# The adapter's large weight in 16 half-megabyte loads paced by the LSTM's steps, and its bias loaded after the first step

## What is computed

```python
xz = einsum('ntd,dk->ntk', x, Wx) + b
def step((h, c), xz_t):
    ai, af, ao, ag = split(xz_t + h @ Wh, 4)
    c = sigmoid(af) * c + sigmoid(ai) * tanh(ag)
    h = sigmoid(ao) * tanh(c)
x = x + all h                                   # (16, 256, 256)

n = layernorm(cond) * gamma + beta
hid = gelu(n @ W1 + bias1)                      # (16, 256)
w = hid @ W2 + bias2                            # W2 is 256 x 8192: the large adapter weight
a1, b1, a2, b2 = [t.reshape(16, 256, 8) for t in split(w, 4)]
mid = gelu(x @ base_down + (x @ a2) @ b2.T)     # the rank-8 factors differ for each sequence
out = x + mid @ base_up.T + (mid @ b1) @ a1.T
```

## Time and profile before

| | |
|---|---|
| median of 3 runs (lowest to highest) | 608.72 us (607.85 to 609.86) |
| the profiled execution: its own time, its span | 610.4 us, 608.4 us |
| PE: matmuls busy, share, records | 589.4 us, 97%, 14092 |
| DVE, ACT, POOL busy | 476.1, 375.6, 49.6 us |
| mean granted TensorE clock | 0.992 of full |
| DMA: moved, mean rate | 39.73 MB, 65 GB/s |

### The profile page before, as it was taken

One profiled execution on the slowest core, in us unless ns is written; L12 is line 12 of the kernel. 1 busy time (PEld: TensorE's weight loads), 2 busy tenths in 40 slices (PEclk: granted clock), 3 DMA queues, 4 the chain that ended last, 5 costly groups with the idle time before them and its releaser, 6 DMA issues.

```text
span 608.4 us, 33942 instructions
## 1 busy us (share of the span) xinstructions
PE 589.4 (97%) x14092; PEld 437.7 (72%) x14092; DVE 476.1 (78%) x2549; ACT 375.6 (62%) x2154; POOL 49.6 (8%) x96
## 2 busy tenths in 40 slices
PE   8697999999999999999999999999999999999997
PEld 5564667777777777777777777777777777777886
DVE  2576787888888888888888888888888888888773
ACT  1364566666666666666666666666666666666663
POOL 5001320000000000000000000000000000000000
PEclk9799899999999999999999999999999999999999
DMA  7889340232322123333212233321223333123301
GB/s 193 218 222 307 62 59 13 38 56 56 56 56 39 39 37 56 55 56 56 42 38 34 56 56 55 55 48 34 34 54 56 56 55 53 32 31 46 56 20 29
DMA packets 32139, 39.73 MB, mean 65 GB/s; under 512 B 3905, under 2 KB 29809, under 8 KB 30962
## 3 DMA queue, kind: packets, MB, share of 16 engines
q1 hardware_dynamic: 31282, 36.51, 30.7%
q0 software_dynamic: 704, 1.05, 1.1%
HBM read 16.05 MB, written 4.19 MB: 33 GB/s over the span
## 4 chain that ended last, share of the span: by engine, by line
PE 95%; issue 1%; DMA 1%; POOL 1%; DVE 1%; SPq 0%; ACT 0%; POOLq 0%; ACTq 0%
PE z L676 36%; PE x_bank L480 19%; PE z_o L676 9%; PE aux L506 8%; PE out_bank L530 7%; PE aux L491 3%; PE aux L458 3%; PE out_bank L562 2%; PE aux L513 2%; PE out_bank L605 2%; DMA seed<-proj 1%; PE out_bank L551 1%; PE x_bank L551 1%; PE x_bank L506 0%; DMA x_nat<-in_x 0%
## 5 line engine op out<-in xcount | busy, mean ns | idle before, releaser
L676 PE MATMUL z<-wh,h_t 128*16 128x96 f32 x8160 | 237.2, 249 | 3.7 <-issue 3.3
L676 PEld LDWEIGHTS z<-wh,h_t 128*16 128x16 f32 x8160 | 152.8, 96 | 112.4 <-DVE h_t L849 80.4
L829 DVE STREAM_TRANSPOSE z<-z 128x96 f32<-128x96 f32 x512 | 152.6, 298 | 73.9 <-PE z L676 50.0
L401 ACT ACTIVATE gates<-z 128x48 f32<-128x48 f32 x512 | 107.6, 210 | 123.2 <-DVE z L829 123.0
L480 PE MATMUL x_bank<-wx,x_t 128*128 128x256 f32 x512 | 156.6, 394 | 0.5 <-ACT x_t L333 0.5
L339 ACT ACTIVATE z<-seed 128x96 f32<-128x96 f32 x512 | 127.5, 249 | 5.8 <-DMA seed<-proj 5.8
L676 PE MATMUL z_o<-wh,h_t 128*16 128x64 f32 x4080 | 104.9, 219 | 0.3 <-issue 0.3
L839 DVE SCALAR_TENSOR_TENSOR prod<-gates 128x32 f32<-128x32 f32 x512 | 98.1, 192 | 0.0
L343 ACT ACTIVATE z_o<-seed 128x64 f32<-128x64 f32 x256 | 58.3, 228 | 60.3 <-DVE h_t L849 60.3
L844 DVE SCALAR_TENSOR_TENSOR gates<-prod 128x16 f32<-128x16 f32 x512 | 84.6, 165 | 8.7
L480 PEld LDWEIGHTS x_bank<-wx,x_t 128*128 128x128 f32 x512 | 81.3, 197 | 6.0 <-issue 1.7
(11 more groups left out here) (123 smaller groups left out, 441.7 us busy)
## 6 DMA issues: line engine op xcount, KB each, us to landing
seed<-proj SPq DMA_DIRECT2D x128, 128.0 KB, 4.3
w<-in_L_cond_W SPq DMA_DIRECT2D x4, 2048.0 KB, 10.7
x_nat<-in_x SPq DMA_DIRECT2D x32, 128.0 KB, 4.3
out<-y_nat SPq DMA_DIRECT2D x32, 128.0 KB, 4.3
wx<-in_L_cond_Wx SPq DMA_DIRECT2D x2, 512.0 KB, 5.5
wh<-in_L_cond_Wh SPq DMA_DIRECT2D x2, 256.0 KB, 6.9
wh<-in_L_cond_Wh SPq DMA_DIRECT2D x1, 512.0 KB, 5.9
w_bias<-in_L_cond_bias POOLq DMA_DIRECT2D x4, 128.0 KB, 6.0
```

The source lines that it names most:

```text
L401: act.activation(gates[s % 2][m][:, 0:3 * B].rearrange("p (g b) -> p g b", b=B), zt[m].rearrange("p (g c) -> p g c", c=C)[:, :, 0:B], ACT. ...
L676: ins = pe.matmul(dst, h_prev[:, kc, :], rhs, start=False, stop=(kc == 1), skip_group_check=True)
L829: dve.transpose(zt[m], z_bank[m][:, 0:GC]).then_inc(turned[m], 1)
```

## The change

W2 is loaded in 16 pieces of 512 KB, one for each piece of work on PE, so that each piece has its own semaphore and PE waits for each. The first two (`W_AHEAD`) go out where the first quarter did. Of the others, piece p is issued once step p - 2 has its h. A piece is a half of the columns and a half of the contraction of a quarter; each of the 128 partitions gets four runs of 1 KB. The bias transfers of POOL now wait until step 0 has its h; they stand behind the `pow` of the layer norm (L959). The cut diff:

```diff
+W_AHEAD = 2
...
-        w2_loaded = [sem(f"w2_loaded{q}") for q in range(4)]
+        w2_loaded = [[sem(f"w2_loaded{q}_{i}") for i in range(NQ)] for q in range(4)]
...
-            w2_q = W2.rearrange("(k p) (q n) -> q p k n", p=P, q=4)
-            def load_w2(q):
-                sp.dma_start(w2[q][:, :, :], w2_q[q]).then_inc(w2_loaded[q], 16)
+            w2_parts = W2.rearrange("(k p) (q j h n) -> q h k p j n", p=P, q=4, j=NQ, n=W_HALF)
+            def load_w2(piece):
+                n, i = divmod(piece, NQ)
+                q, (h, kc) = QUARTERS[n], divmod(i, 2)
+                if piece == 3 * NQ:
+                    sp.wait_ge(w_psum, 2)
+                sp.dma_start(w2[q][:, kc, :].rearrange("p (j h n) -> p h j n", j=NQ, n=W_HALF)[:, h], w2_parts[q, h, kc])\
+                  .then_inc(w2_loaded[q][i], 16)
...
-            load_w2(QUARTERS[0])
+            for piece in range(W_AHEAD):
+                load_w2(piece)
             load_seed(Blk(0, 1))
...
-                if not k.at_least(1):
-                    load_w2(QUARTERS[1])
-                if k.k == 1:
-                    sp.wait_ge(w_psum, 2)
-                    load_w2(QUARTERS[3])
+                for s in range(TB):
+                    piece = k.k * TB + s + W_AHEAD
+                    if piece < 4 * NQ:
+                        sp.wait_ge(ht_ready[1], k.k * TB + s + 2)
+                        load_w2(piece)
                 if front:
                     load_seed(k.plus(2))
-                if not k.at_least(1):
-                    load_w2(QUARTERS[2])
...
-                    if i == 0:
-                        pe.wait_ge(w2_loaded[q], 16)
+                    pe.wait_ge(w2_loaded[q][i], 16)
...
-            bias_q = bias2.rearrange("(q j n) -> j q n", q=4, j=NQ)
-            for j in range(NQ):
-                pool.dma_start(w_bias[32 * j:32 * j + B, :, :], bias_q[j].partition_broadcast(B))\
-                    .then_inc(w_bias_loaded, 16)
             pool.wait_ge(ln_step, 6)
             pool.tensor_tensor(c_stat[:, 4:5], c_stat[:, 3:4], neg_half[:, :], ALU.pow).then_inc(ln_pow, 1)
...
+            pool.wait_ge(ht_ready[1], 2)
+            bias_q = bias2.rearrange("(q j n) -> j q n", q=4, j=NQ)
+            for j in range(NQ):
+                pool.dma_start(w_bias[32 * j:32 * j + B, :, :], bias_q[j].partition_broadcast(B))\
+                    .then_inc(w_bias_loaded, 16)
```

## The result

The change makes the kernel slower: 615.45 us (614.34 to 616.11, 4 runs) against 609.19 for the kernel before on the same chip, a recorded ratio of 1.0093 with a 95% interval of 1.0076 to 1.0111 (the two medians alone give 1.0103). The forecast was 603.1 with a range to 612.3, so the time lies outside. The profiled span went from 608.4 to 613.7 us, by 5.3.

What follows compares the result with a forecast made beforehand. PE bounds the kernel, with three stops for late instruction fetches behind W2's loads. All stops go, 5.65 us, everything else costed 0: 608.72 - 5.65 = 603.1 us, range 602.3 to 612.3.

Steps and rivals of the forecast that it cites:

- What bounds the kernel: PE, busy 97% of the span; three stops between steps 7 and 15 are late instruction fetches, costing 5.65 us.
- the stops: PE's three stops: all go if a fetch waits only for the running transfer, 5.65 us gained, chance 0.55.
- only for the transfer that is running on its DMA engine: PE's instruction fetch waits at most a piece, a seed transfer or both; with the fetch 4.0 us, under 5.1.
- the queue decides: Rival: PE's fetch waits for all issued ahead; stops of 2.0 and 4.8 us, slower at 613.0 us; chance 0.26.
- the fetch itself: Time PE's instruction fetch needs once the load ahead is through: 42.85 - 41.6 = 1.25 us.
- the case at 88.2: PE's packet crossing at record 1482: fetch read as coming after all four seed transfers, counted for the queue rival.
- the forecast's own sum for the running transfer: Longest fetch wait on PE: piece 1.34 us, seed transfer 1.4, fetch 1.25, together 4.0 of 5.1 us.
- The bias at nothing: POOL's four bias transfers moved behind step 0: cost 0 at both places, covered by eight steps before DVE's first use.
- The pacing: SP's issue of W2: pieces 2 to 5 back to back from about 32.9, then from piece 7 one a step.
- The rate of the pieces: W2's 1 KB runs taken at 391 GB/s, as Wx and Wh moved, giving a piece in 1.34 us.
- PE's waits and SP's issues at nothing: Twelve more waits on PE and twelve more issues on SP, about 0.63 us each, beside PE: cost 0.

Runs made afterwards that it cites:

- the spread schedule: Kernel before, bias early, W2 in 16 transfers: four at the first quarter's place, others behind steps 3-6, 9-14, 16, 17; 0.9936 with 1 KB runs.
- the pieces alone: Kernel before with W2 loaded in the change's 1 KB pieces at its issue points, but the bias left early; 614.01 us, 1.0066.

## Why the prediction was wrong

- **What bounds the kernel** was read rightly: the three stops are late fetches of PE's program. The grid of 126 records holds in the change too (344, 470, 596, 722), the stops vanish with W2's loads, and they can be made at will with useless ones. Their price of 5.65 us compares with 6.1 us of span in the run without the loads (0.9918 of the time, or 5.0 us).
- **The step that failed** is the one called "the stops": it took it as likelier that a fetch waits "only for the transfer that is running on its DMA engine", and so had all three go. The runs with useless loads show that it waits behind several transfers: four in a row stop PE 11 times, a single one 12 times. In the change 0.93 to 1.40 MB passed ahead of the first late fetch, where the running transfer has at most 0.52. The rival "the queue decides" was right in sign and in the main of the mechanism. Its two stops of 2.0 and 4.8 us were three, of 1.21, 1.91 and 3.41, and its 613.0 us compares with 608.72 x 1.0093 = 614.4. That it came so close is in part luck: it let a fetch wait for all that is ahead, gave 1.25 us to the fetch itself (below), and had no stop near 57.
- **The fetch was looked for in the wrong packets.** What moves at 42.25 to 42.75, at 60.25 and from 92.25 are the last packets of loads and seeds. The queues from 42.25 to 42.75 hold no fetch, and that of the case at 88.2 is in 90.25 to 90.50:

```profile
q1 hardware_dynamic: 2, 0.02, 7.9%
...
q1 hardware_dynamic: 31, 0.03, 118.0%
q8 instruction: 1, 0.02, 45.0%
```

The four seeds there land at 88.6, 89.7, 91.0 and 91.8, so this fetch did pass between them: the row that the prediction counted against its forecast was none. A second term falls with this reading, the 1.25 us "for the fetch itself". From the window in which the late fetches start (41.00, 47.75 and 58.00 here; 40.25, 51.50 and 58.50 before) to PE's going on it takes 2.1 to 3.0 us, which leaves 2.1 to 3.0 of the 5.1 us for waiting, and not 3.9. With it the forecast's own sum for the running transfer is 1.34 + 1.4 + 2.1 to 3.0 = 4.8 to 5.7 us, no longer safely under 5.1.
- The Trainium skill's rule ("DMA: Bandwidth & Descriptors", section "Queues, rings and completion order"), that an engine takes turns between its queues at each packet of typically 9 to 17 descriptors, would have let the fetch in within one piece. The trace does not agree with that number: 1428 packets of q1, nearly all runs of 1 KB and 89 for each of 16 engines, passed between 36.50 and 41.00 ahead of the fetch, and 941, or 59 for each, from 38.30 on. The page's ceiling of 64 is not excluded by this.
- **The bias at nothing** was wrong too. The place it leaves was costed rightly: the 4.73 us of the seeds did not move. But only the wait for the bias itself was looked at in its new place, and not what is queued beside it: 0.41% alone, 0.9% in the spread schedule, 0.27% on top of the pieces (1.0066 to 1.0093). The intervals of the last pair overlap.
- **The pacing** was seen in the main: pieces do go out in a row at 33.5, eight and not four. Without that row the price of the pieces alone is gone (1.0066 to 1.0002). That one piece a step is too dense beside the seeds was not seen, though it can be estimated: at 345 GB/s a piece takes 1.52 us of each 2.24, or 0.68, and the seeds 5.6 us of each block of 8 x 2.24 = 17.9, or 0.31, 0.99 together.
- **The rate of the pieces** was mis-sized: 391 GB/s against about 345 (351 at 43 to 44). With 4 KB runs the time is the same within the intervals, so no part of the price is shown to hang on this.
- **PE's waits and SP's issues at nothing** held as prices: no wait of PE for a piece of W2 shows in the trace after, and the seeds' delay to 44.31 is covered, though an issue took 1.3 us and not 0.63.

What stays open is the exact order: why so much goes ahead of a fetch in the change, while a part of a load that was issued before it comes behind it in the kernel before. No run here measures what sets its place.

## What to carry to other kernels

Where an engine stops without waiting for anything, count its instructions up to each stop. Distances that are multiples of what one packet of the instruction queue holds point to late fetches, and any transfer, however unrelated, can then be the cause. Look up in which window the fetch itself moves before you say what it waited for. Cutting a big load into pieces does little by itself; what helped here is that the queue is short when a fetch is due. So work out the share of the DMA engines that pieces and regular traffic need together, leave steps out beside the regular bursts, and look at what in front of the issuing engine makes its gates pass all at once. A transfer moved from an idle gap into a full stretch can cost even if its consumer is far away.

## What the runs showed of the hardware that was not expected

- Transfers to 32 partitions moved some 200 GB/s with all engines at work, against 345 to 426 for the same bytes to 128 partitions; seeds and bias, to 16 partitions, some 76 to 136. For W2's loads, the number of partitions written mattered far more than the length of the runs.
- SP's issue of a piece took from 0.37 to 2.10 us. In the changed kernel, single pieces (start us, us, line, operation):

```profile
33.54 1.79 SPq L278 DMA_DIRECT2D w<-in_L_cond_W  x1
...
37.02 2.10 SPq L278 DMA_DIRECT2D w<-in_L_cond_W  x1
...
54.68 0.37 SPq L278 DMA_DIRECT2D w<-in_L_cond_W  x1
```

What makes the difference is not shown. Full engines alone do not: from 54 to 55 their share is 1.09, and the issue takes 0.37 us.
- PE has at most one packet of 16 KB ahead: in the change it stands on the grid of 126 records until the fetch that moved last is there (from 41.00 to 41.25 for the stop that ends at 43.78, from 47.75 to 48.00 for the one that ends at 50.79). The Trainium skill ("Runtime: NRT & Kernel Launch", section "Instruction fetch mechanics") has the sequencer fetch the next page while it executes the current one, with which the trace agrees, and calls the crossing mostly hidden; the stops of up to 3.77 us do not agree.
